# FFN's input by way of DRAM with positions on partitions, and LayerNorm applied after the products

## The chip, the cores and the metric

One core of a Trainium2 chip. The time is that of one execution on the device in microseconds, the median over runs. Engines: TensorE (PE; its weight loads are PEld), VectorE (DVE), ScalarE (ACT), GpSimd (POOL), and SyncE (SP), which here only issues DMAs.

## What is computed

```
for each of 16 samples b (x[b]: 128 channels x 1024 positions, ctx[b] the same shape):
  h  = layernorm(x[b])                                   # over the 1024 positions
  q  = softmax over the 64 rows of each head (Wq h) / 8  # 8 heads of 64
  k  = softmax over positions (Wk ctx);  v = Wv ctx
  o  = Wo (k v^T applied to q) + bo                      # 128 x 1024
  o  = o / max(norm of o over channels, 1e-12) * g * sqrt(128)
  x1 = x[b] + o                                          # X after the residual
  h2 = layernorm(x1)                                     # over the 1024 positions
  units = gelu(h2 Wu1^T + bu1) Wu2^T;  query = h2 Wq'^T  # 256 and 64 columns: 320 in one product
  gate  = from units and var(h2), with a mean over all samples
  top 8 of 256 slots by (query Wr^T)(keys Wr^T)^T, softmax of their logits, values Wvd^T Wvu^T
  out[b] = x1 + h2 + gate * that
```

Everything is float32. Products that need it are made of three float32r products of high and low parts: (high, high), (low, high), (high, low).

## The kernel before

X (all 16 samples, 128 x 16 x 1024) stays in SBUF, channels on partitions. The kernel is written engine by engine, with the order of each engine's instructions fixed by hand and semaphores between them. A loop of 19 periods (b), each of four steps (i), pipelines the attention: in period b the keys of sample b are made, the queries of p = b - 1, the output of o = b - 2, and of e = b - 3 the output is normalised, turned and added to X.

- The output of o_pair has positions on partitions (o_sb, 128 positions x 8 blocks x 128 channels). norm_scale (GpSimd, step 1) clamps and takes the power of the sums of squares and scales o_sb by rn. o_turn (TensorE, step 2) turns it into `turn`, channels on partitions. For e < 13 ScalarE's o_scale reads `turn`, times gs = g sqrt(128) per partition, back into o_sb, and GpSimd's residual adds it to X; for the last three VectorE's residual does both. rstd2_pow (GpSimd) makes rstd2, nb2 = -mean rstd and 1 + rstd of the second LayerNorm.
- The FFN's first half runs for each sample as a hidden_step. Steps 0 to 7 lie in the last two periods (b = 17 and 18, beside the end of attention), 8 to 16 behind them. Step b of each engine: ScalarE: hT_high(b+1), unit_gelu(b-1), h_scale(b+2), unit_sum(b-1). TensorE: h_transpose(b+1), hidden_products(b), and from step 9 on query_transpose of two samples. VectorE: hT_low(b+1), unit_weights(b-1), unit_bias(b), query_rows(b), query copies. GpSimd: hidden_sum(b).
- h_scale writes h2 = X rstd2 + nb2 to hbuf (channels on partitions). h_transpose turns its eight 128 x 128 blocks by TensorE into k_slot or q_slot in PSUM; hT_high rounds that to float32r (hT_hi) and hT_low subtracts to get hT_lo. hidden_products makes 24 products of 320 columns with WuqT_hi and WuqT_lo. hidden_sum writes X := X (1 + rstd2) + nb2, the part of the output that needs no gate.
- Wuq_in (1280 KB) is loaded on ScalarE's queue in period 16 when the key products are done; ScalarE rounds it to WuqT_hi, and VectorE makes WuqT_lo (in its queue ahead of q_reciprocal(15, 2)). SP's queue loads x and ctx, issues the moves of keys (move_k), writes q_turned (q_out) and loads the FFN's tables; ScalarE's queue reads q_turned back (q_in).
- From tile 15's products on, a tail: scores, top 8, softmax, value products and output, 16 samples of it.

In the trace's lines: o_pair is L548, g_part L517, m_product L526, q_turn L501, o_turn L559, h_transpose L591, hidden_products L604, query_transpose L611; q_scale L1067, norm_scale L1078 to L1082, residual L1088, hidden_sum L1116, WvuT_lo L1187, mt_bias L1073; hT_low L1287, unit_bias L1293, unit_weights L1304; h_scale L876, hT_high L882, q_exponential L800, q_copy L805, o_copy L835.

## Time and profile before

| | |
|---|---|
| runs | 623.72, 620.17, 623.61 us; median 623.61 |
| profiled execution | 622.58 us, its span 620.8 us |
| mean granted TensorE clock | 0.996 |
| busy | PE 592.5 us (95%), PEld 516.5 (83%), DVE 541.1 (87%), ACT 418.1 (67%), POOL 409.7 (66%) |
| DMA | 106.11 MB, mean 171 GB/s |

The profile is of one execution; times in it are counted from the span's start. Busy time is the sum of an engine's instructions; the clock is what TensorE was granted, as a share of its full 2.4 GHz. Attention alone takes the stretch to about 480 us, the FFN's first half lies from there to 572, and the tail behind it.

### The profile page before, as it was taken

How to read it: one execution, taken by the hardware profiler on the slowest of the kernel's cores; microseconds unless marked ns; L12 is line 12 of the kernel's file. 1: busy time of each engine (PE TensorE's matmuls, PEld its weight loads, DVE VectorE, ACT ScalarE, POOL GpSimd, SP SyncE). 2: the span in 40 equal slices, each digit the busy share in tenths (PEclk: the TensorE clock that was granted, in tenths of full speed). 3: DMA queues.
4: the chain of work that ended last, by engine and by line, in shares of the span. 5: the costliest groups of instructions: out<-in, count | busy, mean ns of one | idle time of the engine just before them, and what ended most of it. 6: DMA issues, size and time to landing. Idle time of an engine off the chain costs nothing.

```text
span 620.8 us, 11452 instructions
## 1 busy us (share of the span) xinstructions
PE 592.5 (95%) x3718; PEld 516.5 (83%) x3718; DVE 541.1 (87%) x721; ACT 418.1 (67%) x864; POOL 409.7 (66%) x421
## 2 busy tenths in 40 slices
PE   4999999999999999999999999999989799999896
PEld 3778888888888888888888888888878799998574
DVE  5999999999999999999999999999968544866996
ACT  5566667676777676767676676777666576584783
POOL 4964457787767768687878787767655735430494
PEclk9999999999999999999999999999999899999999
DMA  8849695868687685959595868676563600000156
GB/s 315 223 128 231 189 248 167 216 180 207 188 201 212 171 231 154 243 173 242 162 243 169 219 179 204 197 195 175 134 196 109 180 8 2 2 2 0 59 214 271
DMA packets 63530, 106.11 MB, mean 171 GB/s; under 512 B 11392, under 2 KB 43680, under 8 KB 61168
## 3 DMA queue, kind: packets, MB, share of 16 engines
q1 hardware_dynamic: 52576, 84.32, 46.4%
q10 hardware_dynamic: 10000, 18.62, 13.2%
q0 software_dynamic: 896, 2.45, 1.3%
q8 instruction: 30, 0.49, 0.4%
q14 instruction: 28, 0.23, 0.1%
HBM read 46.62 MB, written 25.17 MB: 116 GB/s over the span
## 4 chain that ended last, share of the span: by engine, by line
PE 83%; DVE 4%; DMA 3%; ACT 3%; issue 3%; POOL 2%; ACTq 1%; DVEq 0%; SPq 0%; POOLq 0%
PE ob L548 18%; PE gm L517 16%; PE gm L604 5%; PE q_slot L475 4%; PE turn L501 4%; PE k_slot L477 4%; PE k_slot L475 4%; PE q_slot L477 4%; PE k_slot L476 4%; PE q_slot L476 4%; PE turn L604 4%; PE gm L526 2%; PE turn L559 2%; DMA Wuq_in<-Wuq_cols 2%; PE turn L734 1%
## 5 line engine op out<-in xcount | busy, mean ns | idle before, releaser
L1067 POOL TENSOR_TENSOR qs_sb<-qs_sb,qrec 128x1024 f32<-128x1024 f32 x64 | 122.0, 1906 | 96.3 <-DVE qrec L1257 96.1
L548 PEld LDWEIGHTS ob<-mt_sb,q_hd 128*128 128x128 f32 x1024 | 124.3, 194 | 8.3 <-ACT q_hd L805 3.0
L548 PE MATMUL ob<-mt_sb,q_hd 128*128 128x128 f32 x1024 | 127.9, 279 | 2.4 <-ACT q_hd L805 2.4
L517 PE MATMUL gm<-ekT,ctxT 128*128 128x256 f32 x512 | 118.2, 379 | 0.0
L517 PEld LDWEIGHTS gm<-ekT,ctxT 128*128 128x128 f32 x512 | 95.9, 190 | 13.6
L800 ACT ACTIVATE qs_sb<-qs_sb 128x1024 f32<-128x1024 f32 x64 | 67.9, 1061 | 47.3 <-DVE qs_sb L1246 45.9
L790 ACT ACTIVATE ek<-k_slot,nkm 128x1024 f32<-128x1024 f32 x62 | 69.1, 1114 | 32.7 <-DVE nkm L1221 32.5
L1221 DVE TENSOR_REDUCE nkm<-k_slot 128x1 f32<-128x1024 f32 x62 | 74.0, 1194 | 13.9 <-PE k_slot L477 13.9
L1253 DVE TENSOR_REDUCE qsum<-qs_sb 128x16 f32<-128x1024 f32 x64 | 77.1, 1205 | 7.6 <-ACT qs_sb L800 6.5
L1246 DVE TENSOR_TENSOR qs_sb<-q_slot,qm 128x1024 f32<-128x1024 f32 x64 | 78.4, 1224 | 2.2
L1228 DVE STREAM_TRANSPOSE kt<-ek 128x1024 f32<-128x1024 f32 x64 | 79.0, 1234 | 1.1 <-DMA ekT<-kt 1.1
L1240 DVE TENSOR_REDUCE qm<-q_slot 128x16 f32<-128x1024 f32 x64 | 76.0, 1187 | 0.5 <-issue 0.5
L475 PE MATMUL k_slot<-ctx_hi,WkT_hi 128*128 128x512 f32 x124 | 54.7, 441 | 9.3 <-DVE ctx_lo L1419 7.1
L475 PE MATMUL q_slot<-WqT_hi,xn_hi 128*128 128x512 f32 x128 | 53.0, 414 | 2.3 <-DVE qs_sb L1246 2.3
L1061 POOL TENSOR_TENSOR xn_lo<-xn,xn_hi 128x1024 fp32r<-128x1024 f32 x16 | 38.3, 2396 | 20.2 <-ACT xn_hi L784 20.2
L477 PE MATMUL q_slot<-WqT_lo,xn_hi 128*128 128x512 f32 x128 | 50.3, 393 | 0.0
L476 PE MATMUL q_slot<-WqT_hi,xn_lo 128*128 128x512 f32 x128 | 50.0, 391 | 0.0
L477 PE MATMUL k_slot<-ctx_lo,WkT_hi 128*128 128x512 f32 x124 | 49.3, 398 | 0.0
L476 PE MATMUL k_slot<-ctx_hi,WkT_lo 128*128 128x512 f32 x124 | 49.1, 396 | 0.0
L796 ACT COPY g_sb<-gm 128x512 f32<-128x512 f32 x16 | 9.4, 587 | 54.6 <-PE gm L517 54.6
L845 ACT ACTIVATE junk<-o_sb 128x128 f32<-128x128 f32 x128 | 37.6, 297 | 4.8 <-issue 4.7
L1266 DVE STREAM_TRANSPOSE qt<-qs_sb 128x1024 f32<-128x1024 f32 x32 | 38.0, 1188 | 0.0
(208 smaller groups left out, 1309.9 us busy)
## 6 DMA issues: line engine op xcount, KB each, us to landing
ekT<-kt SPq DMA_DIRECT2D x488, 64.0 KB, 2.9
q_turned<-qt SPq DMA_DIRECT2D x16, 1024.0 KB, 4.8
q_hd<-q_turned ACTq DMA_DIRECT2D x64, 256.0 KB, 5.7
ctx_in<-ctx_rows SPq DMA_DIRECT2D x16, 512.0 KB, 6.1
x_all<-x SPq DMA_DIRECT2D x16, 512.0 KB, 4.7
ctxT<-ctx_cols SPq DMA_DIRECT2D x16, 512.0 KB, 5.5
out<-q_hd SPq DMA_DIRECT2D x15, 512.0 KB, 2.6
Wuq_in<-Wuq_cols ACTq DMA_DIRECT2D x1, 1280.0 KB, 9.3
```

The lines of the kernel that those rows point to most:

```text
L475: nc.tensor.matmul(dst, lhs[0], rhs[0], start=True, stop=False)
L476: nc.tensor.matmul(dst, lhs[1], rhs[0], start=False, stop=False)
L477: return nc.tensor.matmul(dst, lhs[0], rhs[1], start=False, stop=True)
L517: last = nc.tensor.matmul(gm[:, cols], ctxT[:, b % 2, j, :], ekT[:, 2 * half:2 * half + 2, :, j * BLK:(j + 1) * BLK], start=(j == 0), stop ...
L548: last = nc.tensor.matmul(ob[:, (j % 4) * C:(j % 4 + 1) * C], q, mt_sb[:, b % 2, t, :], start=(t == 0), stop=(t == T - 1))
L790: nc.scalar.activation(ek[:, i % 2, :], k_psum(b, i)[:, :], ACT.Exp, bias=nkm[:, i:i + 1], accum_out=ksum[:, b % 2, i:i + 1]).then_inc(k_e ...
L1067: nc.gpsimd.tensor_tensor(e, e, qrec[:, i % 2, :].unsqueeze(2).broadcast_to([P, PAIR, DH]), ALU.mult).then_inc(q_mul, 1)
L1221: V.tensor_reduce(nkm[:, i:i + 1], k_psum(b, i)[:, :], AX, ALU.max, negate=True).then_inc(k_max, 1)
L1228: V.transpose(kt[:, i, :], ek[:, i % 2, :]).then_inc(k_T, 1)
L1240: V.tensor_reduce(qm[:, :], q, AX, ALU.max).then_inc(q_max, 1)
L1246: V.tensor_tensor(qs_sb[:, i % 2, :].rearrange("p (m d) -> p m d", d=DH), q, qm[:, :].unsqueeze(2).broadcast_to([P, PAIR, DH]), ALU.subtra ...
L1253: V.tensor_reduce(qsum[:, :], qs_sb[:, i % 2, :].rearrange("p (m d) -> p m d", d=DH), AX, ALU.add).then_inc(q_sum, 1)
```

## The change

h2 is no longer made and turned before the products. Instead:

- o_sb is multiplied by g sqrt(128) while positions are still on partitions: g is loaded as a row, broadcast to all partitions, and norm_scale gets one more GpSimd pass (o_final). o_scale and residual then use `turn` without gs.
- o_store (ScalarE's queue, step 2) writes each o_sb to DRAM (o_turned, 512 KB a sample). x_cols, a second copy of x with positions on partitions in the same order, is a new input; Wuq's rows are permuted to that order.
- For each sample SP loads x_cols[n] into hx (three buffers) and o_turned[n] into ho (two), and GpSimd's h_add sums them: x1 with positions on partitions, not normalised. hT_high and hT_low read hx in SBUF where they read PSUM before.
- LayerNorm is applied to the products: h2 W = rstd (x1 W) - mean rstd (column sums of W). column_sums (TensorE, 16 products with a matrix of ones) makes the sums, ScalarE copies them (colsum), GpSimd's unit_shift makes shift = colsum nb2 + bu1 for each sample, and unit_bias and query_rows scale by rstd2 and add shift in one operation.
- hidden_sum moves from GpSimd to ScalarE, in h_scale's place; h_transpose and its PSUM use go, so products, scores and query transposes get other PSUM places, and query_transpose now follows one sample at a time from step 1 on.
- In GpSimd's order ctx_low moves from step 1 to behind q_scale in step 2. SP's order gets the loads of hx and ho, the first three ahead of q_out(15).

```diff
+        raw = Wuq_in[:, :, :].rearrange("p j u -> p (j u)")
+        WvuT_in, colsum = raw[:, 0:N], raw[:, N:N + UQ]
+        shift = raw[:, N + UQ:N + 3 * UQ].rearrange("p (k u) -> p k u", k=2)
+        bu1, Wu2 = raw[:, N + 3 * UQ:N + 4 * UQ], raw[:, N + 4 * UQ:N + 4 * UQ + UH]
         WuqT = [sb(f"WuqT{s}", [P, J, UQ], F32R, ffn) for s in ("_hi", "_lo")]
-        q_rows = sb("q_rows", [P, B, P], scope=ffn)
-        hbuf = sb("hbuf", [P, 2, N], scope=ffn)
-        bu1 = sb("bu1", [P, UH], scope=ffn)
+        hx = sb("hx", [P, HX, N], scope=ffn)
+        ho = sb("ho", [P, 2, N], scope=ffn)
+        q_rows = sb("q_rows", [P, 2, P], scope=ffn)
...
+            def load_hx(n):
+
+                wait(sp, hT_lo_done, n - HX + 1)
+                sp.dma_start(hx[:, n % HX, :], x_cols[n]).then_inc(hx_in[n % HX], 16)
+
+            def load_ho(n):
+
+                wait(sp, h_added, n - 1)
+                sp.wait_ge(o_stored[n % 2], 16 * (n // 2 + 1))
+                sp.dma_start(ho[:, n % 2, :], o_turned[n]).then_inc(ho_in[n % 2], 16)
+
             def ffn_tables():
-                for half in range(2):
-                    sp.wait_ge(k_moved[half], moved(B))
-                sp.dma_start(bu1[:, :], bu1_row.broadcast_to([P, UH])).then_inc(ffn_in, 16)
+                sp.wait_ge(wuq_lo, 1)
+                sp.dma_start(bu1[:, 0:UH], bu1_row.broadcast_to([P, UH])).then_inc(bu1_in, 16)
+                sp.wait_ge(q_prod, 4 * B)
+                load_ho(1)
...
+                if b == B:
+                    for half in range(2):
+                        sp.wait_ge(k_moved[half], moved(B))
+                    load_hx(0)
+                    load_ho(0)
+                    load_hx(1)
...
+            for n in range(2, B):
+                if n > 2:
+                    load_hx(n)
+                load_ho(n)
...
-                pe.wait_ge(o_scaled, b + 1)
+                pe.wait_ge(o_final, b + 1)
...
-            def h_transpose(b, k):
-                pe.wait_ge(h_done, b + 1)
-                wait(pe, hT_hi_done, b - 1)
-                wait(pe, hT_lo_done, b - 1)
-                for j in range(J):
-                    last = nc.tensor.transpose(slot[k][:, j * P:(j + 1) * P], hbuf[:, k, j * P:(j + 1) * P],
-                                               ident[:, :])
-                last.then_inc(h_T, 1)
+            def column_sums():
+                pe.wait_ge(k_exp, 4 * B)
+                pe.wait_ge(wuq_hi, 1)
+                pe.wait_ge(wuq_lo, 1)
+                for c in range(2):
+                    for j in range(J):
+                        last = nc.tensor.matmul(colsum_psum, ones[:, :].bitcast(F32R), WuqT[c][:, j, :],
+                                                start=(c == 0 and j == 0), stop=(c == 1 and j == J - 1))
+                last.then_inc(colsum_prod, 1)
 
             def hidden_products(b, k):
                 pe.wait_ge(hT_hi_done, b + 1)
                 pe.wait_ge(hT_lo_done, b + 1)
-                before = b if b < EARLY else b - 1
-                wait(pe, units_biased, before)
-                wait(pe, rows_copied, before)
+                if b == 1:
+                    pe.wait_ge(colsum_done, 1)
+                wait(pe, units_biased, b - 1)
+                wait(pe, rows_copied, b - 1)
...
             def hidden_step(b):
-                if b + 1 < B:
-                    if b == 0:
-                        pe.wait_ge(q_sub, 4 * B)
-                    h_transpose(b + 1, (b + 1) % 2)
+                if b == 0:
+                    column_sums()
...
+                    hidden_products(b, b % 2)
+                if b > 0:
+                    query_transpose(b - 1, (b - 1) % 2)
...
             def o_scale(b):
 
                 act.wait_ge(o_T, b + 1)
-                act.wait_ge(gs_done, 1)
+                act.wait_ge(o_stored[b % 2], 16 * (b // 2 + 1))
                 wait(act, nm2_done, b - 1)
                 nc.scalar.activation(o_sb[:, b % 2, :, :].rearrange("p j c -> p (j c)"), turn[:, :], ACT.Copy,
-                                     scale=gs[:, :], accum_out=osum[:, b % 2:b % 2 + 1]).then_inc(o_back, 1)
+                                     accum_out=osum[:, b % 2:b % 2 + 1]).then_inc(o_back, 1)
+
+            def o_store(b):
+
+                act.wait_ge(o_final, b + 1)
+                nc.scalar.dma_start(o_turned[b], o_sb[:, b % 2, :, :].rearrange("p j c -> p (j c)")).then_inc(
+                    o_stored[b % 2], 16)
 
             def square_sum(b):
 
@@ -870,16 +895,17 @@
...
-            def h_scale(b, k):
+            def hidden_sum(b):
+
                 act.wait_ge(nb2_done, b + 1)
-                wait(act, h_T, b - 1)
-                nc.scalar.activation(hbuf[:, k, :], X[:, b, :], ACT.Identity, bias=nb2[:, b, :],
-                                     scale=rstd2[:, b, :]).then_inc(h_done, 1)
+                act.wait_ge(one_rstd2_done, b + 1)
+                nc.scalar.activation(X[:, b, :], X[:, b, :], ACT.Identity, bias=nb2[:, b, :],
+                                     scale=one_rstd2[:, b, :]).then_inc(y_done, 1)
 
             def hT_high(b, k):
-                act.wait_ge(h_T, b + 1)
+                act.wait_ge(h_added, b + 1)
                 wait(act, units_prod, b - 1)
-                nc.scalar.copy(hT[0][:, k, :, :], slot[k][:, :].rearrange("p (j c) -> p j c", j=J)).then_inc(hT_hi_done, 1)
...
-                if b + 2 < B:
-                    h_scale(b + 2, b % 2)
+                if has(b):
+                    hidden_sum(b)
...
                     if i == 2:
+                        if has(e):
+                            o_store(e)
...
+                pool.wait_ge(o_scaled, b + 1)
+                pool.wait_ge(g_scaled, 1)
+                nc.gpsimd.tensor_tensor(o_sb[:, b % 2, :, :], o_sb[:, b % 2, :, :],
+                                        g_bc[:, :].unsqueeze(1).broadcast_to([P, J, C]), ALU.mult).then_inc(o_final, 1)
...
-            def hidden_sum(b):
-
-                pool.wait_ge(h_done, b + 1)
+            def h_add(b):
+
+                pool.wait_ge(hx_in[b % HX], 16 * (b // HX + 1))
+                pool.wait_ge(ho_in[b % 2], 16 * (b // 2 + 1))
+                nc.gpsimd.tensor_tensor(hx[:, b % HX, :], hx[:, b % HX, :], ho[:, b % 2, :], ALU.add).then_inc(h_added, 1)
+
+            def unit_shift(b):
+
+                if b == 0:
+                    pool.wait_ge(colsum_done, 1)
+                    pool.wait_ge(bu1_ready, 1)
+                    pool.wait_ge(bu1_in, 16)
                 pool.wait_ge(nb2_done, b + 1)
-                pool.wait_ge(one_rstd2_done, b + 1)
-                nc.gpsimd.tensor_scalar(X[:, b, :], X[:, b, :], one_rstd2[:, b, :], nb2[:, b, :], ALU.mult,
-                                        ALU.add).then_inc(y_done, 1)
+                wait(pool, rows_copied, b - 1)
+                nc.gpsimd.tensor_scalar(shift[:, b % 2, :], colsum[:, :], nb2[:, b, :], None, ALU.mult).then_inc(shift_scaled, 1)
+                pool.wait_ge(shift_scaled, b + 1)
+                nc.gpsimd.tensor_tensor(shift[:, b % 2, :], shift[:, b % 2, :], bu1[:, :], ALU.add).then_inc(shift_done, 1)
 
             nc.gpsimd.memset(half_neg[:, :], -0.5).then_inc(consts, 1)
             nc.gpsimd.memset(ones[:, :], 1.0).then_inc(consts, 1)
@@ -1150,11 +1189,11 @@
                         residual(e - 1)
                     if i == 3 and 0 < b < B:
...
+                    if i == 2 and b > 0 and has(b + 1):
+                        ctx_low(b + 1)
...
+                        h_add(0)
+                    if early_step(b, i) == 0:
+                        pool.wait_ge(q_prod, 4 * B)
                         nc.gpsimd.memset(q_rows[:, :, BOT:P], 1.0).then_inc(query_ones, 1)
-                    if early_step(b, i) > 0:
-                        hidden_sum(early_step(b, i))
+                        pool.wait_ge(wuq_lo, 1)
+                        nc.gpsimd.memset(bu1[:, UH:UQ], 0.0).then_inc(bu1_ready, 1)
+                    if early_step(b, i) >= 0:
+                        h_add(early_step(b, i) + 1)
+                        unit_shift(early_step(b, i))
             rstd2_pow(B - 1)
 
...
-                V.tensor_tensor(hT[1][:, k, :, :], slot[k][:, :].rearrange("p (j c) -> p j c", j=J),
+                V.tensor_tensor(hT[1][:, k, :, :], hx[:, b % HX, :].rearrange("p (j c) -> p j c", j=J),
                                 hT[0][:, k, :, :].bitcast(F32), ALU.subtract).then_inc(hT_lo_done, 1)
 
             def unit_bias(b, k):
                 dve.wait_ge(units_prod, b + 1)
+                dve.wait_ge(shift_done, b + 1)
+                dve.wait_ge(rstd2_done, b + 1)
                 wait(dve, learned_done, b - 1)
-                V.tensor_tensor(units[:, k, :], unit_psum(b)[:, 0:UH], bu1[:, :], ALU.add).then_inc(units_biased, 1)
-
-            def query_rows(b):
-                V.tensor_copy(q_rows[:, b, 0:BOT], unit_psum(b)[:, UH:UQ]).then_inc(rows_copied, 1)
+                V.scalar_tensor_tensor(units[:, k, :], unit_psum(b)[:, 0:UH], rstd2[:, b, :], shift[:, k, 0:UH],
+                                       ALU.mult, ALU.add).then_inc(units_biased, 1)
+
+            def query_rows(b, k):
+                wait(dve, rows_T, b - 1)
+                V.scalar_tensor_tensor(q_rows[:, k, 0:BOT], unit_psum(b)[:, UH:UQ], rstd2[:, b, :], shift[:, k, UH:UQ],
+                                       ALU.mult, ALU.add).then_inc(rows_copied, 1)
 
             def query_copy(b, k):
...
+                if has(b - 1):
+                    query_copy(b - 1, (b - 1) % 2)
```

## Rows read from the trace of the kernel before

**Rows 1.** The page, part 1: busy us, share of the span, instructions.

```profile
PE 592.5 (95%) x3718; PEld 516.5 (83%) x3718; DVE 541.1 (87%) x721; ACT 418.1 (67%) x864; POOL 409.7 (66%) x421
```

**Rows 2.** Chain that ended last, in time: start us, us, engine, tile, line.

```profile
486.59 3.58 PE ob L548 x16
...
502.49 3.52 PE gm L604 x24
506.01 1.78 PE ob L548 x16
...
514.85 0.87 PE q_slot L591 x8
...
568.32 3.53 PE turn L604 x24
```

**Rows 3.** Groups by line: busy us, mean ns of one, idle before.

```profile
L1088 POOL TENSOR_TENSOR x_all<-x_all,o_sb 128x1024 f32<-128x1024 f32 x13 | 30.9, 2376 | 0.0
L1082 POOL TENSOR_TENSOR o_sb<-o_sb,rn 128x1024 f32<-128x1024 f32 x16 | 30.5, 1908 | 1.3
...
L1080 POOL TENSOR_TENSOR rn<-l2c,half_neg 128x8 f32<-128x8 f32 x16 | 26.8, 1677 | 1.3
...
L1116 POOL TENSOR_SCALAR x_all<-x_all,one_rstd,nb 128x1024 f32<-128x1024 f32 x16 | 20.0, 1251 | 16.0 <-ACT hbuf L876 16.0
...
L1287 DVE TENSOR_TENSOR hT_lo<-k_slot,hT_hi 128x1024 fp32r<-128x1024 f32 x8 | 9.8, 1221 | 3.1 <-ACT hT_hi L882 2.9
...
L1073 POOL TENSOR_TENSOR mt_sb<-mt_sb,bo_bc 128x128 f32<-128x128 f32 x16 | 7.3, 457 | 1.3 <-ACT mt_sb L870 1.2
```

**Rows 4.** Timeline of GpSimd, 480 to 500 us: start us, us, engine, line.

```profile
481.75 0.23 POOL L1100 TENSOR_SCALAR mv<-ssq 128x1 f32<-128x1 f32 x1
...
483.47 0.21 POOL L1109 TENSOR_SCALAR one_rstd<-rstd 128x1 f32<-128x1 f32 x1
...
486.97 1.90 POOL L1067 TENSOR_TENSOR qs_sb<-qs_sb,qrec 128x1024 f32<-128x1024 f32 x1 [0.78 <-DVE qrec L1257]
```

**Rows 5.** Timeline of VectorE, 538 to 548 us.

```profile
538.01 0.76 DVE L1304 TENSOR_TENSOR units<-units,Wu 128x256 f32<-128x256 f32 x1
...
541.44 2.65 DVE L1304 TENSOR_TENSOR units<-units,Wu 128x256 f32<-128x256 f32 x1
...
546.71 0.41 DVE L1304 TENSOR_TENSOR units<-units,Wu 128x256 f32<-128x256 f32 x1
```

**Rows 6.** Timeline of GpSimd in the same stretch.

```profile
537.29 4.17 POOL L1116 TENSOR_SCALAR x_all<-x_all,one_rstd,nb 128x1024 f32<-128x1024 f32 x3
541.43 2.38 POOL L1187 TENSOR_TENSOR WvuT_lo<-WvuT_in,WvuT_hi 128x1024 fp32r<-128x1024 f32 x1
```

**Rows 7.** Timeline of ScalarE, 480 to 487 us.

```profile
481.92 1.01 ACT L882 CAST hT_hi<-k_slot 128x1024 fp32r<-128x1024 f32 x1 [1.34 <-PE k_slot L591]
...
483.31 1.07 ACT L800 ACTIVATE qs_sb<-qs_sb 128x1024 f32<-128x1024 f32 x1
485.53 1.01 ACT L805 COPY q_hd<-turn 128x1024 f32<-128x1024 f32 x1 [1.15 <-PE turn L501]
```

**Rows 8.** The page, part 6: DMA issues, KB each, us to landing.

```profile
x_all<-x SPq DMA_DIRECT2D x16, 512.0 KB, 4.7
...
Wuq_in<-Wuq_cols ACTq DMA_DIRECT2D x1, 1280.0 KB, 9.3
```

**Rows 9.** Timeline of GpSimd in an attention period.

```profile
381.97 1.90 POOL L1082 TENSOR_TENSOR o_sb<-o_sb,rn 128x1024 f32<-128x1024 f32 x1
```

**Rows 10.** Timeline of TensorE in the same period.

```profile
387.26 1.04 PE L559 MATMUL turn<-ident,o_sb 128*128 128x128 f32 x8
```

**Rows 11.** Windows: us, busy of PE, PEld, DVE, ACT, POOL, then the clock.

```profile
464.00:468.00 4.00, 2.11 (x17) 1.86 (x16) 3.29 (x5) 2.99 (x5) 1.93 (x2) 1.00 0.97 214
483.00:486.50 3.50, 1.09 (x8) 0.86 (x8) 3.50 (x4) 2.35 (x4) 3.09 (x6) 0.99 0.62 188
486.50:490.00 3.50, 3.41 (x16) 3.41 (x17) 0.35 (x2) 2.34 (x10) 2.86 (x3) 0.52 0.45 159
```

More of the change, by code:

```diff
@@ L22 @@
 YB = 4
+HX = 3
 BY_VECTOR = 4
@@ L313, in attention_ffn_kernel @@
         o_scaled = sem("o_scaled")
+        o_final = sem("o_final")
+        o_stored = [sem(f"o_stored{k}") for k in range(2)]
         o_T = sem("o_T")
@@ L332, in attention_ffn_kernel @@
         normv_step = sem("normv_step")
-        h_done = sem("h_done")
+        hx_in = [sem(f"hx_in{k}") for k in range(HX)]
+        ho_in = [sem(f"ho_in{k}") for k in range(2)]
+        h_added = sem("h_added")
+        colsum_prod = sem("colsum_prod")
+        colsum_done = sem("colsum_done")
+        shift_scaled = sem("shift_scaled")
+        shift_done = sem("shift_done")
+        bu1_ready = sem("bu1_ready")
         y_done = sem("y_done")
-        h_T = sem("h_T")
         hT_hi_done = sem("hT_hi_done")
@@ L940, in _ @@
                         move_last()
-                    if b == B + 1 and i == 0:
-                        h_scale(1, 1)
                     if 0 < b < B:
@@ L987, in _ @@
                         nc.scalar.dma_start(Wuq_in[:, :, :], Wuq_cols).then_inc(wuq_in, 16)
-                    if b == B and i == 3:
-                        for half in range(2):
-                            act.wait_ge(k_moved[half], moved(B))
-                        h_scale(0, 0)
+                    if early_step(b, i) == 0:
+                        act.wait_ge(colsum_prod, 1)
+                        nc.scalar.copy(colsum[:, :], colsum_psum).then_inc(colsum_done, 1)
                     if early_step(b, i) >= 0:
@@ L1165, in _ @@
                         norm_scale(e)
-                    if i == 1 and b > 0 and has(b + 1):
-                        ctx_low(b + 1)
                     if b == B and i == 3:
@@ L1183, in _ @@
             for b in range(EARLY, B):
-                hidden_sum(b)
+                if b + 1 < B:
+                    h_add(b + 1)
+                unit_shift(b)
                 if b == EARLY + 2:
@@ L1537, in layouts @@
         "bo_row": row("L0_xattn_bo"),
-        "g_col": a["L0_xattn_g"].reshape(C, 1),
-        "Wuq_cols": tiles(np.concatenate([a["L0_ffn_Wu1"].T, a["L0_ffn_Wq"].T], axis=1)),
+        "g_row": row("L0_xattn_g"),
+        "Wuq_cols": tiles(np.concatenate([a["L0_ffn_Wu1"].T, a["L0_ffn_Wq"].T], axis=1)[order]),
         "Wvd_cols": tiles(a["L0_ffn_Wvd"].T),
```

92 lines of the change are left out of this document (35 added, 57 removed).

## The prediction

> **What bounds the kernel now.** I read the page's busy shares first: TensorE works for 95% of the span [rows 1]. That is an average, so the chain of waits comes next, and in its time order only over the end of the program, where the change does most of its work. The chain runs on TensorE nearly without a break from 490 to 572 us. Each FFN tile is there as a pair: eight transposes of the normalised tile, 0.87 us, and 24 products, 3.52 us; the last products (tile 15) start at 568.32 and end at 571.85 [rows 2]. Nothing else is on the chain, so a TensorE instruction removed there is a gain until another engine is late. The profiled execution took 622.58 us for a span of 620.8; the median of the three runs is 623.61, so 622.58 is a fair base and 1.0 of the difference is noise.
>
> **Part 1, removed: 16 x 8 transposes.** 16 x 0.87 = 13.9 us of TensorE [rows 2]. Added there: 16 column-sum products as wide as the FFN products. 24 of those take 3.52, so one takes 0.147 and 16 take 2.35. TensorE alone would gain 11.6 us. A tile then needs 3.52 and one query transpose (0.87 / 8 = 0.11), 3.65 us of it. The question is whether the others can deliver a tile in 3.65.
>
> **Part 2, GpSimd's new work.** Per tile it loses the output sum over X (1.25 in the mean) and gains h_add, a two-input pass over 1024 (2.38, the residual's own duration), and unit_shift. That is 320 wide: the scaling lies between 0.21 for one column and 1.2 for 1024, so 0.53; the addition between 0.46 (128 wide) and 2.38 (1024), so 0.87 [rows 3, 4]. With gaps 1.45. Together 3.85 per tile where 1.25 was: already longer than TensorE's 3.65. Each normalisation of an attention output also gets a second pass (times g). Its nearest rows are 1.91 (the pass before it, broadcast along the inner axis) and 2.38 (two plain inputs); its inner axis is read plainly, so I take 2.38. One norm_scale is then 1.68 + 1.91 + 2.38, and 0.45 for the clamp and gaps: 6.4 [rows 3]. Two of them, for tiles 14 and 15, stand between h_adds in GpSimd's queue.
>
> **Part 3, the price that the diff does not show.** The low part hT_low reads PSUM and SBUF today and takes 1.22 whatever GpSimd does [rows 3]. Afterwards both inputs (hx and the high part) lie in SBUF. The kernel has one such operation in this stage, the product with Wu2 at L1304. Its plain duration is 0.41, but the one at 541.44 took 2.65: it ended at 544.09, just after GpSimd's 2.38 us pass that began at 541.43 [rows 5, 6]. The one at 538.01 took 0.76: it waited for the first of three GpSimd passes to end, and the three took 4.17 instead of 3 x 1.2 [rows 5, 6]. So a two-SBUF-input VectorE operation and a GpSimd pass exclude each other, for whole instructions. I call this the exclusion. Per tile it then holds h_add 2.38 + shift 1.40 + hT_low 1.20 + Wu2 product 0.42 = 5.4 us, where the removed pair and its small change took 4.4 to 4.6 on TensorE.
>
> The Trainium skill says the same ("SBUF — State Buffer", "SBUF: two separate sides"): the port pair that VectorE and GpSimd share is an exclusive lock for a whole instruction, taken by a VectorE operation with two SBUF inputs against a GpSimd one that reads SBUF. By that rule, which these rows bear out, the tile costs 5.4; if hT_low escaped it, 3.85.
>
> **Part 4, the start of the stage.** ScalarE's cast of tile 0 stands ahead of the copy, exponential and q_copy that release the o_pair at 486.59 [rows 2, 7]. Today it waits for TensorE's early transposes and starts at 481.92. Afterwards it waits for h_add(0), which GpSimd reaches only after rstd2_pow(12), done at 483.68 [rows 4]: 483.7 + 2.4 = 486.1. Then cast 1.0, copy 0.55 (the exponential follows the cast's end of 482.93 by 0.4, behind that copy), exponential 1.05, q_copy 1.0 [rows 7]: 489.7; o_pair 1.8, column sums 2.35: 493.9; their copy 0.45. Meanwhile hT_low(0), the row sum and q_scale(15,3) (1.90, at 486.97 today [rows 4]) queue up one behind another, and h_add(1) ends at about 494.8. Tile 0's products start at 493.9, not 491.05 (2.9 later). What stops TensorE after that is GpSimd: shift(0) 1.45, norm_scale(14) 6.4, h_add(2) 2.4 give 505.1, and tile 2's products start at 507.8 against 502.5.
>
> **The sum.** From 494.8 to the end of h_add(15) GpSimd has 14 h_adds (33.3), 15 shifts (21.8), two norm_scales (12.8), three rstd2_pow (4.9: the one from 481.75 to 483.68 took 1.93, and these lack its first operation of 0.23 [rows 4]) and WvuT_lo (2.38), with gaps 77. VectorE adds to the exclusion 14 low parts (16.8) and 13 Wu2 products (5.5), 22.3; I let 6 of it lie beside GpSimd's tiny operations and powers, since no row shows that these exclude anything. h_add(15) ends at 494.8 + 77 + 16.3 = 588.1. Behind it: cast 1.0, low part 1.2, products 3.5, and 3.6 of waiting (shift(14), and the cast stands behind a ScalarE sum that waits for the Wu2 product), so 597.4 against 571.85: 25.6 late. Before the stage, 1.5 MB of hx and ho are asked for while Wuq_in (1280 KB, 9.3 us to landing, and the chain waits for it) is in flight [rows 8]. It is between 0 (they come later in the rings) and 4 us (they share equally, and 512 KB take 4.7 in traffic [rows 8]); I take 2. The tail saves two query copies, 0.5. Moving hidden_sum to ScalarE costs nothing: it takes the place of h_scale, a pass of the same size. 622.6 + 25.6 + 2.0 - 0.5 = 649.7; I say 649.
>
> **What I cost at nothing.** In the attention stage nothing leaves TensorE, so nothing is gained. The g pass moves o_turn's input from 383.9 to 386.3, TensorE's o_turn starts at 387.26 [rows 9, 10]: 0.9 spare. If the cover failed it would be some 0.3 us in each of 13 periods, 4 us. ctx_low moves behind q_scale, with 3 us to its reader. o_store waits on ScalarE for o_final, ahead of g_copy, the exponential and the casts; ScalarE idles there for the G products today. In SP's queue hx and ho stand ahead of q_out(15), whose data come 15 us later. Landing of hx and ho: 4.7 against the 6.8 us that two buffers give at 5.4 per tile.
>
> **The rivals.** (a) *The exclusion does not reach hT_low; GpSimd alone paces.* For: the 3.85 holds anyway; hT_low might slip between passes. Against: 2.65 at L1304 [rows 5], an operation of the same form. Without the 16.3 h_add(15) ends near 572 to 574, and TensorE, held up on the way, ends 9 to 11 late: 632 to 635. (b) *Faster.* TensorE stays the bound, with the place in the FFN stage, the price 11.6 less the 2.9 at the start: 614. It decides if the exclusion holds under 3.65 per tile. For it speaks only that ScalarE and VectorE have room; against it, h_add would have to be near 0.6, and every two-input row of GpSimd over 1024 says 1.9 or 2.4 [rows 3]. (c) *The clock.* TensorE worked 1.09 of the 3.5 us to 486.5, then the granted clock was 0.52 (1.2 GHz for nearly all of it) and an o_pair took 3.58 instead of 1.78 [rows 2, 11]. With 1.8 idle per tile it may fall now and then; but 464 to 468, half idle, kept 1.00 (2.4 GHz) [rows 11]. At half clock a tile is 7.2, past 5.4 by 1.8: over eight late tiles 14 us, 663; half of that, 656. (d) *The attention stage loses its 0.3 per period*, or the tables come 4 late: 653 to 656. (e) *No effect*: transposes gone, GpSimd later by the same amount, 617 to 629; it needs the exclusion absent and GpSimd's passes a tenth shorter.
>
> **How the numbers follow.** Forecast (643 to 653): 0.66. (a) 0.11. (c) 0.08, (d) 0.08. (b) 0.03, (e) 0.04. The forecast's own width: g pass at 1.91 and the shift at 1.2 instead of 1.4 take 3.6 off, Wuq moves it by 2 each way. The range reaches down to (a)'s upper half and up to half of (c): 635 to 658. A difference under 1% (6.2 us) can hardly be told from none in this kernel. Faster by over 1%: 0.03; within 1%: (e) and a corner of (a), 0.05; slower by over 1%: 0.92.
>
> **What would show it.** GpSimd over 90% busy from 484 to 590; mean hT_low well over 1.22, with single ones near 3.5, and h_add over 2.38 in the mean; L1304's successor likewise; TensorE idle about 1.8 us per tile, released by hT_low; tile 15's products ending near 599; the periods of attention still about 29 us and the 49 us after the last products nearly unchanged. Wrong if hT_low stays at 1.2, if GpSimd's passes over 1024 come out short, or if the FFN tiles follow at 3.7.

## The result, and the profile after

| | median of runs | lowest to highest | ratio to before (95% interval) |
|---|---|---|---|
| before (run beside it) | 622.52 | 620.17 to 623.72 | |
| after | 655.69 | 654.91 to 656.79 | 1.054 (1.050 to 1.058) |

The changed kernel is 5.4% slower. Its profiled execution took 654.92 us for a span of 653.1. The forecast was 649, the range 635 to 658. Two executions of what follows are left out: the profiled one of e8, which ran at a granted clock of 0.748 from end to end and took 758 us, and one of the kernel before beside e9 to e11, which took 1545. Line numbers from here on are those of the changed kernel.

The page's busy shares of after, against [rows 1]:

```profile
PE 594.1 (91%) x3606; PEld 515.4 (79%) x3606; DVE 549.9 (84%) x721; ACT 418.9 (64%) x865; POOL 509.6 (78%) x470
```

TensorE has 112 instructions fewer (128 transposes gone, 16 column-sum products added) and is as busy as it was, at a mean granted clock of 0.968 in place of 0.996; GpSimd has 100 us more. Windows of after (us from the start, busy of PE, PEld, DVE, ACT, POOL with instructions, granted clock, DMA share, GB/s):

```profile
60.00:440.00 380.00, 380.00 (x2400) 333.19 (x2399) 362.27 (x394) 268.66 (x570) 307.98 (x296) 1.00 0.82 215
...
500.00:510.00 10.00, 7.66 (x59) 7.45 (x57) 2.69 (x6) 1.41 (x2) 9.68 (x6) 1.00 0.62 151
...
550.00:560.00 10.00, 6.52 (x44) 6.00 (x42) 6.52 (x17) 3.24 (x7) 7.07 (x9) 1.00 0.46 152
560.00:570.00 10.00, 5.79 (x28) 5.58 (x29) 6.77 (x8) 5.50 (x8) 9.83 (x6) 0.66 0.46 157
570.00:580.00 10.00, 7.30 (x49) 6.78 (x47) 4.30 (x9) 3.52 (x7) 9.92 (x6) 1.00 0.46 158
```

In the attention stage (60 to 440) TensorE is busy for all of 380 us, as before: the g pass, 27 us more of GpSimd there, is hidden. The loss is in the FFN stage, where GpSimd is 94.7 us busy of the 100 from 500 to 600 and TensorE 73.5 (5.8 to 8.6 of each 10 us, and all 10 from 520 to 530 only). The chain of waits of after, a late tile of it (start us, us, engine, tile, line), answers to [rows 2]:

```profile
583.72 2.56 POOL hx L1144
586.28 1.06 POOL Wuq_in L1154
587.34 0.04 issue
587.42 0.07 POOL Wuq_in L1156
587.49 1.81 issue
589.30 2.59 POOL hx L1144
```

The chain now walks along GpSimd alone: h_add, the shift's scaling, the shift's addition, next h_add, 5.58 us a tile. (The 1.81 that the view calls issue are the rest of the addition, which the next rows show to last 1.92.) TensorE is not on it. The same stretch on the timeline (start us, us, engine, line), GpSimd and VectorE, as [rows 5, 6] were read:

```profile
583.72 2.56 POOL L1144 TENSOR_TENSOR hx<-hx,ho 128x1024 f32<-128x1024 f32 x1
...
586.25 1.08 POOL L1154 TENSOR_SCALAR Wuq_in<-Wuq_in,nb 128x320 f32<-128x320 f32 x1
...
587.39 1.22 DVE L1331 TENSOR_TENSOR hT_lo<-hx,hT_hi 128x1024 fp32r<-128x1024 f32 x1 [2.34 <-ACT hT_hi L908]
587.42 1.92 POOL L1156 TENSOR_TENSOR Wuq_in<-Wuq_in 128x320 f32<-128x320 f32 x1
```

hT_low starts at 587.39, in the gap between GpSimd's two shift operations, and ends at 588.61. The addition, started 0.03 later, takes 1.92 where it takes 0.86 with nobody beside it: it lasts longer by 1.06, and hT_low had 1.19 of its time left. That is the exclusion, but here GpSimd pays and VectorE goes first. The groups of GpSimd from 484 to 600 (busy us, mean ns of one | idle before), against [rows 3]:

```profile
L1144 POOL TENSOR_TENSOR hx<-hx,ho 128x1024 f32<-128x1024 f32 x16 | 39.4, 2462 | 0.0
L1156 POOL TENSOR_TENSOR Wuq_in<-Wuq_in 128x320 f32<-128x320 f32 x15 | 26.0, 1732 | 1.3
L1154 POOL TENSOR_SCALAR Wuq_in<-Wuq_in,nb 128x320 f32<-128x320 f32 x15 | 16.8, 1120 | 1.8 <-ACT Wuq_in L1016 1.8
L1111 POOL TENSOR_TENSOR o_sb<-o_sb,g_bc 128x1024 f32<-128x1024 f32 x2 | 4.7, 2366 | 0.2
```

Between the first h_adds and the last, GpSimd waits twice: 1.8 us for the column sums (the row of L1154), and 2.6 us, ahead of h_add(9), for the statistics of tile 15's X, which stand behind unit_bias(7) in VectorE's order:

```profile
557.62 0.22 POOL L1131 TENSOR_SCALAR ve<-mv 128x1 f32<-128x1 f32 x1 [2.60 <-DVE mv L1326]
```

And the two operations of VectorE that have both inputs in SBUF, from 480 to 610 (duration ns min/median/max, first and last start):

```profile
L1331 DVE TENSOR_TENSOR hT_lo<-hx,hT_hi x16: 1216/1226/1930, 489.1 to 598.6; 128x1024 fp32r<-128x1024 f32 x16
...
L1353 DVE TENSOR_TENSOR units<-units,Wuq_in x16: 411/1090/1103, 513.2 to 606.3; 128x256 f32<-128x256 f32 x16
```

Wuq_in landed 11.9 us after its issue where [rows 8] show 9.3 (e7 comes back to it):

```profile
Wuq_in<-Wuq_cols ACTq DMA_DIRECT2D x1, 1280.0 KB, 11.9
```

### The profile page after: what moved, and what is told of

Its sections match the earlier page's. It is cut to its first block, busy times and chain, and to the rows that moved or that the text cites. A ratio compares the mean times of both kernels' runs of the same rounds, so it can differ in the third digit from the quotient of the medians.

```text
span 653.1 us, 11371 instructions
## 1 busy us (share of the span) xinstructions
PE 594.1 (91%) x3606; PEld 515.4 (79%) x3606; DVE 549.9 (84%) x721; ACT 418.9 (64%) x865; POOL 509.6 (78%) x470
## 4 chain that ended last, share of the span: by engine, by line
PE 68%; POOL 14%; issue 5%; DVE 5%; DMA 3%; ACT 3%; ACTq 1%; DVEq 0%; SPq 0%; POOLq 0%
PE ob L579 16%; PE gm L548 15%; POOL hx L1144 6%; PE q_slot L506 4%; PE k_slot L506 4%; PE k_slot L508 4%; PE k_slot L507 4%; PE q_slot L508 4%; PE q_slot L507 4%; PE turn L532 4%; POOL Wuq_in L1154 3%; PE gm L557 2%; DMA Wuq_in<-Wuq_cols 2%; PE turn L590 2%; POOL Wuq_in L1156 2%
## 5 line engine op out<-in xcount | busy, mean ns | idle before, releaser
L548 PEld LDWEIGHTS gm<-ekT,ctxT 128*128 128x128 f32 x512 | 96.0, 190 | 13.6
L637 PE MATMUL k_slot<-WuqT_hi,hT_hi 128*128 128x320 f32 x128 | 44.9, 351 | 25.7 <-issue 25.7
L1331 DVE TENSOR_TENSOR hT_lo<-hx,hT_hi 128x1024 fp32r<-128x1024 f32 x16 | 20.3, 1269 | 54.2 <-ACT hT_hi L908 54.2
L637 PEld LDWEIGHTS k_slot<-WuqT_hi,hT_hi 128*128 128x128 f32 x128 | 27.6, 215 | 28.8 <-issue 28.8
L908 ACT CAST hT_hi<-hx 128x1024 fp32r<-128x1024 f32 x16 | 16.7, 1046 | 45.4 <-POOL hx L1144 45.4
```

Source lines behind the costliest of these rows:

```text
L548: last = nc.tensor.matmul(gm[:, cols], ctxT[:, b % 2, j, :], ekT[:, 2 * half:2 * half + 2, :, j * BLK:(j + 1) * BLK], start=(j == 0), stop ...
L637: last = nc.tensor.matmul(dst[:, 0:UQ], hT[a][:, k, j, :], WuqT[c][:, j, :], start=(j == 0 and n == 0), stop=(j == J - 1 and n == 2))
```

## The experiments

Each is the changed kernel with the edit shown; times are medians, the ratio is to the kernel before on the same chip. "Tile" is the distance of two late h_adds. The median of before beside them was 624.08 (e1 to e4), 622.05 (e5 to e8), 622.60 (e9 to e11) and 621.33 (e12). The kernel after was not run again beside the experiments, so a difference of 1 or 2 us between kernels of different groups can be the chip's.

**e1: hT_low with one input in PSUM** (other data: the low part is not the true one).

```
-  V.tensor_tensor(hT[1][:, k], hx[:, b % HX, :] ..., hT[0][:, k], ALU.subtract)
+  V.tensor_tensor(hT[1][:, k], k_slot[:, k * HALF:k * HALF + C] ... broadcast, hT[0][:, k], ALU.subtract)
```

> The changed kernel, except that hT_low takes its first input from a PSUM bank that holds old products instead of from hx (so the low part that goes into the products is not that of the reference; every instruction, wait and size stays). My theory: hT_low and GpSimd's passes then no longer exclude each other. The second shift instruction (1.90 where hT_low slips in ahead of it, 0.86 alone) goes back to 0.87 in every tile, a late tile takes about 4.6 us instead of 5.55, and over the 15 tiles the time falls by 12 to 16 us, to 640 to 644. Rival, GpSimd's own work alone sets the pace and the exclusion is only seen in passing: the time stays within 2 us of 655.7. Rival, the lowered clock sets it: no change, the products still take 5 to 6 us in half of the tiles.

649.1, ratio 1.040 (1.037 to 1.044). The tile falls from 5.6 to 4.54, as expected of the exclusion, and the addition is nearly free of waits; the time, 640 to 644 in the expectation, does not fall as far:

```profile
L1156 POOL TENSOR_TENSOR Wuq_in<-Wuq_in x16: 857/874/1192, 498.6 to 588.9; 128x320 f32<-128x320 f32 x16
```

The median of L1156 was 1896 in after. The total gained 6.6 us and not more, for of the 12 gained at the end of the last h_add (585.5 against 597.5) 5 were given back behind it. The cast of tile 15 starts 1.9 us after its h_add (587.42), behind a sum for which ScalarE idled 2.8 us, waiting for VectorE; and the products of tile 14 take 5.3 us where a tile at full clock takes 3.5.

**e2: without the g pass** (L1111; g is not applied).

> The changed kernel without GpSimd's second pass in norm_scale: the multiplication of the attention output by g is left out. My theory: the pass is hidden in the attention stage (nothing changes from 60 to 440 us) and counts only where tiles 14 and 15 are normalised between two h_adds, 2 x 2.35 = 4.7 us: 651. Rival, the attention stage pays for it: 0.3 us in each of 13 periods more, 645 to 648, and the stretch of TensorE's 2400 products before 440 us ends earlier. Rival, GpSimd isn't the bound: 655.

650.6, ratio 1.044 (1.041 to 1.046). The attention stage has nothing to gain: TensorE is 380.0 of 380 us busy in it. The 5 us are the size of the two passes of 2.37 that stand in GpSimd's queue between the FFN's tiles, and the expected 651 came. The traces give it less cleanly: the first h_add starts 1.6 earlier here than in after (484.01 against 485.61, within a scatter that e7 describes), and the distances across the two normalisings are 2.2 and 1.4 shorter (11.40 for 13.56, 9.63 for 11.06). The late tiles stay at 5.4 to 5.6. GpSimd's passes are on the path of the stage.

**e3: ten more products of 320 columns on TensorE** in each of the steps 8 to 13, written to a free PSUM region and not used.

> The changed kernel with ten more products of 320 columns (1.5 us at full clock) on TensorE after each tile's products in steps 8 to 13, into a PSUM place that nobody reads. My theory, the clock falls because TensorE waits and isn't why it waits: the granted clock rises from 0.66 to 0.72 in windows of 550 to 590 to over 0.9, and the time stays within 1.5 us of 655.7. Rival, the half clock is part of the 6 us by which the kernel is over my 649: the products of the slow tiles take 3.5 instead of 6.4 us and the time falls by 4 to 8 us.

655.0, ratio 1.050 (1.048 to 1.052): unchanged. The granted clock of 560 to 570 and 580 to 590 rose, if not to the 0.9 expected:

```profile
560.00:570.00 10.00, 5.75 (x30) 5.77 (x31) 6.50 (x8) 5.50 (x8) 9.83 (x6) 0.83 0.46 157
```

from 0.66 in after, and GpSimd's row (9.83) did not move. The h_adds follow each other as in after, to within 0.1 us from step to step from h_add(2) on, though TensorE is now busy for all of 570 to 580 and 590 to 600. Up to the last h_add the clock is a result of TensorE's waiting and no cause of the time.

**e4: the scaling as a two-operand form.**

```
-  nc.gpsimd.tensor_scalar(shift, colsum, nb2[:, b], None, ALU.mult)
+  nc.gpsimd.tensor_scalar(shift, colsum, nb2[:, b], zero[:, :], ALU.mult, ALU.add)
```

> The changed kernel, with unit_shift's scaling written as multiply and add of a zero from a one-column tile, the form that hidden_sum had before (1.2 us for 1024), in place of the multiplication alone, which takes 1.08 for 320. If the form is what makes 320 columns cost 1.08, the scaling takes 0.5 to 0.6 and the time falls by 15 x 0.5 = 7 to 8 us, to 648, and then that term of the sum was my miss. If it is a price of 320 columns whatever the form, nothing changes.

652.2, ratio 1.046 (1.044 to 1.047), 3.5 less than after and not the 7 to 8 expected. 0.31 a tile were to be had at the median:

```profile
L1155 POOL TENSOR_SCALAR Wuq_in<-Wuq_in,nb,zero x16: 607/774/1908, 498.9 to 594.7; 128x320 f32<-128x320 f32 x16
```

It takes 0.77 at the median against 1.09 for the one-operand form: the multiply with an addition of zero is the faster instruction. But with the scaling shorter, hT_low no longer comes in the gap behind it (1.94 in the mean):

```profile
571.76 2.41 POOL L1235 TENSOR_TENSOR WvuT_lo<-Wuq_in,WvuT_hi 128x1024 fp32r<-128x1024 f32 x1
571.96 3.30 DVE L1334 TENSOR_TENSOR hT_lo<-hx,hT_hi 128x1024 fp32r<-128x1024 f32 x1 [0.73 <-ACT hT_hi L909]
574.13 3.39 POOL L1145 TENSOR_TENSOR hx<-hx,ho 128x1024 f32<-128x1024 f32 x1
575.18 2.62 DVE L1356 TENSOR_TENSOR units<-units,Wuq_in 128x256 f32<-128x256 f32 x1
```

hT_low waits here for nearly a whole GpSimd pass (3.30), the h_add behind waits for hT_low (3.39, ending at 577.52 only), and the product with Wu2 for h_add. All three kinds of victim stand in four rows. The last h_add ended 5.7 us earlier than in after (591.8), and 3.7 of that were lost again by tile 15's products.

**e5: e1, and the product with Wu2 of tiles 7 to 13 reads a PSUM region** (other data, in those tiles).

> e1 with one more edit: the product with Wu2 of tiles 7 to 13 reads a PSUM region that holds other data in Wu2's place (wrong values for those tiles, same shapes), so that in these tiles no VectorE operation with two SBUF inputs is left beside GpSimd's passes. Exclusion theory: the scaling of the shift falls from 1.17 us to about 1.08 and the product from 1.19 to about 0.41, and a tile from 4.54 us to 2.34 + 1.08 + 0.87 = 4.3 to 4.4, GpSimd's bare work; the time falls by 1 to 2 us against e1 (649.1), to 647 to 648. Rival, that GpSimd's passes are slow for a reason of their own (DMA writes into the same buffers): the tile stays at 4.5 and the time at 649.

644.2, ratio 1.036 (1.034 to 1.039): 3 to 5 us less than e1 and not 1 to 2. The h_adds start at 570.65, 575.01, 579.38, 583.77: 4.37 a tile, which is 2.34 + 1.08 + 0.87 and gaps, GpSimd's bare work. The late tiles of after, e1 and e5 are thus 5.58, 4.54 and 4.37. The rest of the fall lies behind the tiles: e5's last h_add ended 0.7 later than e1's (586.2), but tile 15's cast started at once, tile 14's products took 3.8 and not 5.3, and tile 15's ended 4.0 earlier (the table of e12).

**e6: h_add over 8 of 1024 columns** (the FFN sees x without the attention's output elsewhere).

> h_add over 8 of 1024 columns only (the FFN's input is then x without the attention's output; loads, waits and everything else as they are). If GpSimd's chain sets the tile: GpSimd's work falls from 4.3 us a tile of its own to some 2.1, TensorE's 2.78 of products + 0.87 for what stays becomes the bound at about 3.65 less the turns, or VectorE/ScalarE's chain; the stage loses 1.7 to 2.5 us a tile and the time is 612 to 622, on the other side of the kernel before (624.1). If the transfers (1 MB a tile by the sync queue) set the tile: h_add's start still waits for them, and the time stays above 640.

632.8, ratio 1.018 (1.014 to 1.021): 23 us less than after, but still 11 more than before, so both expectations fell. Transfers do not set the tile: two h_adds here follow in 2.4. (The 2.78 us that this expectation gives the products of a tile, and the 2.8 of e8's, stand in no row; they take 3.52.) The late tiles follow at 4.3, TensorE nearly always busy; what is lost is lost early (the table of e12 has 4.1 us at tile 0), and there the chain of waits runs through GpSimd's order (start us, us):

```profile
495.69 1.12 POOL L1154 TENSOR_SCALAR Wuq_in<-Wuq_in,nb 128x320 f32<-128x320 f32 x1 [3.77 <-ACT Wuq_in L1016]
...
499.04 1.68 POOL L1105 TENSOR_TENSOR rn<-l2c,half_neg 128x8 f32<-128x8 f32 x1
500.80 1.90 POOL L1107 TENSOR_TENSOR o_sb<-o_sb,rn 128x1024 f32<-128x1024 f32 x1
502.78 2.35 POOL L1111 TENSOR_TENSOR o_sb<-o_sb,g_bc 128x1024 f32<-128x1024 f32 x1
505.09 0.20 POOL L1144 TENSOR_TENSOR hx<-hx,ho 128x8 f32<-128x8 f32 x1
505.29 1.09 POOL L1154 TENSOR_SCALAR Wuq_in<-Wuq_in,nb 128x320 f32<-128x320 f32 x1
```

Tile 1's products were done at 503.0, but its shift stands behind tile 14's normalising (6.4 us), and the products of tile 2 start at 508.5.

**e7: the first loads of hx and ho wait until Wuq_in has landed** (one wait more in SP's queue).

> The first three loads of the FFN's input are held back on the sync queue until Wuq has landed. Theory: the Wuq transfer takes 9.3 us again in place of 11.9, TensorE's queries and all behind them start 2.6 us earlier, and as GpSimd's chain hangs on its first h_add at 485.6, which waits for its own work before it, the time falls by 1 to 2.6 us, to 653 to 654.7. Rival: the first h_add then waits for its data (issue after 460, landing 3.5 us later, but behind the second table), and the time stays at 655.7 or rises by up to 2.

655.1, ratio 1.053 (1.051 to 1.056): no difference. Wuq_in took 9.0 us, h_add(0) started at 484.84 against 485.61, GpSimd's wait for the column sums grew from 1.8 to 2.7, and the last h_add started at 595.9 against 594.9. But a single trace does not carry the 2.6 at the landing: with the loads left where the change has them Wuq_in took 9.1 (e5), 9.3 (e1, e2), 10.3 (e10), 10.9 (e3, e4), 11.0 (e9), 11.4 (e6) and 11.9 us (after), and h_add(0) started anywhere from 484.0 (e2) to 486.5 (e4, e10). What the loads beside it cost is not shown.

**e8: x1 is summed in the attention stage, h_add is gone.** x with positions on partitions is added to o by GpSimd in place of the residual pass, the sum is stored and turned into X, and the FFN loads the sum alone.

```
-  nc.gpsimd.tensor_tensor(X[:, b, :], X[:, b, :], o_sb[...], ALU.add)     # residual, channels on partitions
+  nc.gpsimd.tensor_tensor(o, o, xc[:, :], ALU.add)                        # xc: x, positions on partitions
-  def h_add(b): ...
-  sp.dma_start(ho[:, n % 2, :], o_turned[n])
+  sp.dma_start(hx[:, n % HX, :], o_turned[n])                             # HX = 5
```

> A version with the same result and no h_add: x with positions on partitions is added to the output in the attention stage, where GpSimd's residual pass stood (that pass and its 2.4 us per tile go; the turned sum is written into X directly), the sum is stored, and the FFN stage loads that alone. GpSimd keeps 1.95 us a tile in the FFN stage, TensorE keeps what the change saved (0.87 us a tile). Theory: the FFN stage is bound by TensorE at about 2.8 to 3.65 us a tile, and the time is 608 to 618, faster than both kernels. Rival: the attention stage pays for the turn that now waits a period longer and for the 512 KB loaded beside it (0.3 us a period or more), and ScalarE or VectorE become the bound of the FFN stage at 3.6 us a tile: 620 to 626, no gain over the kernel before.

637.4, 637.4 and 640.2, ratio 1.026 (1.023 to 1.030); no row of it is used. Both expectations missed: it gains 18 on after but loses 15 to before.

**e9: tile 14's normalising ahead of h_add(1) and unit_shift(0)** in GpSimd's queue.

> GpSimd's order at the start of the FFN stage: the passes that normalise tile 14's output (6.4 us with g's pass) stand ahead of h_add(1) and unit_shift(0), where they stood behind them, queued while GpSimd sat idle for the column sums (1.8 us) and before its last q_scale (3.8 us, which stays). If GpSimd's sum of work sets the stage: up to 1.8 us of idle time go, tile 14's turn is earlier and tile 1 and 2 are later, and the time is 653 to 655.7. If it is the order (tile 14's and 15's turns late, and rstd2 with them) that costs: the idle stretch near 550 goes as well, and the time is 649 to 652.

654.6, ratio 1.052 (1.047 to 1.056): the same work in another order, the same time, as the first expectation has it. The wait of 1.8 for the column sums is gone, and from the start of h_add(0) to the end of the last h_add it is 110.3 us where after has 111.9; the idle 2.6 before tile 15's rstd2 stays.

**e10: the scaling on ScalarE.**

```
+  nc.scalar.mul(shift[:, b % 2, :], colsum[:, :], nb2[:, b, :])           # head of each ScalarE step
-  nc.gpsimd.tensor_scalar(shift[:, b % 2, :], colsum[:, :], nb2[:, b, :], None, ALU.mult)
```

> The scaling of the column sums by -mean*rstd (1.08 us on GpSimd, 1.17 with its gap) is done by ScalarE, at the head of each of its steps; GpSimd keeps the add. Theory, that GpSimd's work sets the tile: 15 x 1.17 = 17.5 us go from the end of the last h_add unless TensorE's 3.65 us a tile or VectorE catch up; a tile of GpSimd alone is then 2.5 + 1.9 = 4.3 with the waits for VectorE, against 5.5, and the time is 638 to 643. Rival, that ScalarE's cast now waits behind the scaling and ScalarE (7 of 10 us busy in places) becomes the bound: 648 to 655.

657.0, ratio 1.058 (1.050 to 1.066), above both ranges. 1.17 us a tile left GpSimd and nothing was gained, so GpSimd's bare sum is not the whole bound. A late tile (start us, us):

```profile
587.41 0.87 POOL L1162 TENSOR_TENSOR Wuq_in<-Wuq_in 128x320 f32<-128x320 f32 x1 [2.50 <-ACT Wuq_in L922]
588.24 2.39 POOL L1153 TENSOR_TENSOR hx<-hx,ho 128x1024 f32<-128x1024 f32 x1
...
588.30 3.41 DVE L1337 TENSOR_TENSOR hT_lo<-hx,hT_hi 128x1024 fp32r<-128x1024 f32 x1 [1.10 <-ACT hT_hi L908]
```

With the scaling gone no gap of GpSimd is open when hT_low comes. It starts 0.06 after h_add and takes 3.41: some 2.2 of waiting, then its own 1.2. Behind it on VectorE is the product with Wu2 (0.41), behind that ScalarE's sum, the scaling (0.55), the addition and the next h_add. That ring is 2.4 + 1.1 + 0.4 + 0.3 + 0.6 + 0.9 = 5.7 us, the tile measured (the h_adds start at 582.57, 588.24 and 593.96).

**e11: e8 with the scaling on ScalarE and the order of e9.**

> The version without h_add, with the scaling on ScalarE and the normalising of tiles 14 ahead of the column sums. Its predecessor gave 637.4 to 640.2 without a profile at full clock. Theory, that GpSimd's order at the start and the shift's 2.1 us (with VectorE's waits) were what held it: 620 to 628. Rival, that its attention stage is longer (512 KB more in flight each period, the turn a period later): the FFN stage gets shorter and the time stays at 633 to 638, and the profile shows the attention's periods over 29 us.

636.7, ratio 1.022 (1.018 to 1.026): as e8. The rival's number came, but not for its reason: in the attention stage TensorE is 378.5 of 380 us busy, 1.5 lost and not more. Tile 0's unit_bias starts 7.5 us later than in after: its products end 3.6 later, behind a read back of the queries that took 10.6 us (median) where after has 5.0, and its shift, behind tile 14's normalising on GpSimd, is 4.0 later than these.

**e12: e8 with the whole shift in one VectorE operation,** in the change's order.

```
+  V.scalar_tensor_tensor(shift[:, k, :], colsum[:, :], nb2[:, b, :], bu1[:, :], ALU.mult, ALU.add)
```

> The version without h_add once more, in the change's own order, with each tile's shift (column sums times -mean*rstd, plus bu1) in one VectorE operation of 320 columns in place of GpSimd's two: no operation of GpSimd then stands in a tile's path but the few of its rstd. VectorE has 3 of 10 us free, the operation should take 0.48 us as the like one on units does. Theory (GpSimd's queue delays tiles 1, 2, 5 and the last turn, the rest is TensorE's): the shift of tile 0 no longer holds tile 14's normalising back, tiles come at TensorE's 3.6 us, and the time is 620 to 630, against 636.7 and 638.8 for the two versions before it. Rival, that what is left is the attention stage (378.5 of 380 us busy), the start of the FFN stage, and TensorE's clock at 1.2 GHz after each idle stretch: the time stays at 631 to 637.

632.9, ratio 1.018 (1.014 to 1.022), the fastest of the whole kernels, and still slower than before; the rival's range holds it. When the products of tile 0 ended, and when unit_bias (one operation per tile, behind its products and its shift) started for tile 0 and tile 15:

| | products of tile 0 end | unit_bias, tile 0 | unit_bias, tile 15 | from the first to the last column |
|---|---|---|---|---|
| before | 494.56 | 494.60 | 571.87 | 77.3 |
| after | 501.37 | 501.45 | 604.23 | 102.9 |
| e1 | 500.31 | 500.35 | 597.41 | 97.1 |
| e5 | 500.77 | 500.81 | 593.37 | 92.6 |
| e6 | 498.64 | 498.73 | 580.25 | 81.6 |
| e11 | 505.00 | 508.98 | 585.90 | 80.9 |
| e12 | 505.48 | 507.95 | 581.96 | 76.5 |

In e12 unit_bias of tile 0 comes 2.5 us behind its products, for the one VectorE operation has two inputs in SBUF and is under the exclusion as well:

```profile
504.27 3.24 POOL L1124 TENSOR_TENSOR o_sb<-o_sb,xc 128x1024 f32<-128x1024 f32 x1
505.20 2.66 DVE L1329 SCALAR_TENSOR_TENSOR Wuq_in<-Wuq_in,nb 128x320 f32<-128x320 f32 x1
```

It takes 0.54 or 0.55 in the next two tiles. With GpSimd out of the tile the stage, counted from the products, is 0.8 us shorter than before, and it starts 10.9 later. Its chain of waits:

```profile
463.81 13.36 DMA q_hd<-q_turned
...
535.78 1.06 PE turn L590 x8
536.84 5.05 PE k_slot L638 x24
542.00 3.52 PE k_slot L638 x24
```

The read back of the queries took 13.4 us, with x, x1 and Wuq_in (13.6 us to landing) in flight beside it. The other loss is tile 15's output, which goes through 10.1 us of GpSimd before its turn at 535.78. TensorE waits 4.2 us for it and then runs the next products at a lower clock (0.72 from 536 to 542): 5.05 and not 3.52. Both losses are read from the chain; no run takes them away.

## Why the prediction was right, point by point

The forecast case came about, 5 us above its value (654.9 against the sum of 649.7) by errors of size that cancel in part, and by two waits that the sum does not have.

- **TensorE (part 1).** Right: 112 instructions fewer, and nothing of it is seen in the time. Even e12, with GpSimd out of the tile, is only 0.8 us shorter than before from tile 0's products to tile 15's, a stretch in which 14 transposed tiles, 12.2 us of TensorE, are saved.
- **The shift's price (part 2): the mis-sized term.** I took 0.53 for the scaling, between 0.21 for one column and 1.2 for 1024. But the row of 1.2 is of a two-operand form. The one-operand form takes 1.12 in the mean at 320 columns: 14 x 0.59 = 8.3 us more than in the sum, up to the last h_add. (The sum has 15 shifts there; only 14 stand before h_add(15), so 1.45 us are counted too many.) The two-operand form, once alone at 0.61 (e4), would have been near my number. The addition, 0.87, and h_add, 2.35 alone, were right, as was the g pass (2.37; 6.4 for a norm_scale).
- **The exclusion (part 3).** Shown by e1 and e5: take away VectorE's second SBUF input and the tile falls from 5.58 to 4.54 and 4.37. My 16.3 us up to h_add(15) compare with some 15: the 14 additions there take 24.05 - 14 x 0.87 = 11.9 more than alone, the 14 h_adds 34.70 - 14 x 2.35 = 1.8, and three single ones 1.5 (a scaling of 1.53, WvuT_lo at 2.60, the first operation of a rstd2_pow at 1.08). The last is a tiny operation beside hT_low (511.31 to 513.24), so the tiny ones wait too, and not all of the 6 us that I let lie beside them could. The 5.4 of the tile came out as 5.58 with the scaling 0.55 longer, so the exclusion per tile is less than I took: 1.05 for hT_low and 0.2 for Wu2.
- **Who pays: wrong.** I said hT_low would be well over 1.22, with single ones near 3.5, and named "hT_low stays at 1.2" as a sign of being wrong. Its median is 1.226: the sign came, and yet the exclusion is there, so it was a poor sign. It comes in the gap between the scaling and the addition, and the addition takes 1.9. The Wu2 product took 1.09 and not 0.41, as I had said. With the gap closed or missed (e10, e4) the 3.3 to 3.4 that I had foreseen appear. What a tile costs is nearly the same, 5.58 in after and 5.70 in e10, though GpSimd has 1.17 less to do in e10. TensorE was released by hT_low as I said (in after one ends at 594.23, the products start at 594.33).
- **The start (part 4).** h_add(0) started at 485.61 and ended at 487.96, against my 486.1 + 2 for Wuq_in. With starts from 484.0 to 486.5 in the experiments, a hit within 0.2 is partly luck. h_add(2) ended at 510.1, where I had 505.1 + 2. The 3 us between are a wait of 1.8 for the column sums, the addition of tile 0 at 1.72 and its scaling at 1.11.
- **Wuq_in.** 2.6 for my 2 at the landing, and GpSimd's rstd2_pow(12) ended 1.97 later than in [rows 4] (485.65 against 483.68), as the term had it. But these are one trace against one. With the same loads beside it the landing took 9.1 to 11.9 in the experiments, and e7, which holds them back, gains nothing at the end. The term of 2 is neither shown nor refuted.
- **The end.** h_add(15) ended at 597.5 (588.1 + 2 forecast), tile 15's products at 604.2 (599.4): 6.7 between them, not 9.3. The waiting of 3.6 that I had there did come in e1 (11.9) and e4 (10.4).
- **The balance.** h_add(1) ended at 496.6 (496.8 forecast). From there to the end of h_add(15) it took 100.9 us and not 93.3, 7.6 over: 8.3 for the scaling and 4.4 for the two waits of GpSimd (1.8 for the column sums, 2.6 for tile 15's statistics), which the sum put at nothing, against 1.45 for the shift counted too many, 1.1 on the exclusion and some 2.5 on gaps and passes. With 2.6 too much behind h_add(15) and 0.4 more in the tail the 5.2 us are met. That 649 lay so near is in part luck: errors of 13 us one way met 8 the other.
- **At nothing.** GpSimd was 94.9 of 106 us busy from 484 to 590, just short of my 90%. The attention stage held (380 of 380 busy); the tail is 48.9 us as it was; landing of hx and ho did not matter.
- **Rivals.** (a) and (b) fell with e1 and the tile of 5.58. (c) The clock did fall, to 0.66 in four windows of 10 us (510, 540, 560, 580), and e3 shows that it is off the path up to the last h_add. (d) did not happen. (e) neither. (b) set an h_add under 0.6 us as its condition; e6 has 0.2 and is still 11 us slower than before, so the condition was not enough.

**What stays open.** In e12 the 13.4 us of the read back are seen; which of the transfers beside it must move was not tried, nor was tile 15's output taken off GpSimd. So the 10 us by which e12's profiled execution is slower than before's are read from its chain, but their causes are not shown by a run. Why tile 14's products run at a lower clock in e1 and not in e5 is not shown either.

## What to carry to other kernels

A step taken off the busiest engine is worth nothing if what replaces it lands on an engine that must then do more per tile than the first one did: add up the second engine's tile before counting the saving, its order and what is queued behind its waits included. When an input moves from PSUM to SBUF, count the other engine's passes over the same stretch: VectorE with two SBUF inputs and GpSimd took turns, whole instructions at a time, and it cost 1.2 us in a tile of 5.6. A price read off another form of an instruction (two operands for one) can be wrong by a factor of two, and stands in every tile. And what one trace shows against one other, such as a landing 2.6 us later, is worth little until the traces that should be alike have been compared.
